# A third ring place for the shifted strips of the second convolution, and a second queue for their copies

## What is computed

```python
x = x + L0(gn(x))   # a 3x3 convolution of the 2-D Fourier transform, and back
x = x + L1(gn(x))   # rows of an image kept or dropped by the sign of a dot product
x = x + conv3x3(gn(x), W)         # "first convolution" in this text
x = x + conv3x3(gn(x), weight)    # "second convolution", the stage that is changed
```

## Time and profile before

| | us |
|---|---|
| median of three runs | 4663.69 |
| the profiled execution | 4668.15 |
| its span, from the first to the last instruction | 4666.4 |
| TensorE (PE) busy | 4247.7 (91%) |
| DVE busy | 2763.7 (59%) |
| ACT busy | 2637.1 (57%) |
| DMA queue q1 (SP's), share of the time of 16 DMA engines | 57.5% |
| DMA queue q10 (ACT's) | 0.3% |

### The profile page before, as it was taken

One profiled execution on the slowest core, in us unless ns is written; L12 is line 12 of the kernel. 1 busy time (PEld: TensorE's weight loads), 2 busy tenths in 40 slices (PEclk: granted clock), 3 DMA queues, 4 the chain that ended last, 5 costly groups with the idle time before them and its releaser, 6 DMA issues.

```text
span 4666.4 us, 172858 instructions
## 1 busy us (share of the span) xinstructions
PE 4247.7 (91%) x60064; PEld 2285.3 (49%) x60064; DVE 2763.7 (59%) x9972; ACT 2637.1 (57%) x7597; POOL 3.5 (0%) x22
## 2 busy tenths in 40 slices
PE   4999989999899998998999988999889999888786
PEld 1555436555355544555345543555435554355432
DVE  1677717775277743777357771777717775277730
ACT  4455655556555565555655565556555556544463
POOL 0000000000000000000000000000000000000000
PEclk8999899999999899999999999999899999999998
DMA  7443666646666566665666666565666547544376
GB/s 201 108 126 107 165 159 175 176 133 166 155 177 176 137 163 158 177 176 145 152 166 175 174 154 151 163 176 150 163 152 172 176 136 174 145 123 123 102 182 195
DMA packets 437852, 732.96 MB, mean 157 GB/s; under 512 B 42544, under 2 KB 109296, under 8 KB 437232
## 3 DMA queue, kind: packets, MB, share of 16 engines
q1 hardware_dynamic: 434544, 722.07, 57.5%
q10 hardware_dynamic: 2816, 4.20, 0.3%
HBM read 323.98 MB, written 134.22 MB: 98 GB/s over the span
## 4 chain that ended last, share of the span: by engine, by line
PE 83%; DMA 6%; SPq 3%; issue 3%; DVE 3%; ACT 1%; DVEq 0%; ACTq 0%
PE ps L1332 25%; PE ps L1250 20%; PE ps L1235 19%; PE ps L1243 6%; DMA shared<-x 5%; PE ps L1259 5%; PE ps L1109 5%; SPq L439 1%; SPq L469 1%; DMA x<-x 1%; PE ps L1357 1%; PE ps L1155 1%; PE ps L1156 0%; SPq L391 0%; PE ps L1182 0%
## 5 line engine op out<-in xcount | busy, mean ns | idle before, releaser
L1332 PE MATMUL ps<-x,conv_s 64*32 64x512 f32 x12288 | 1401.4, 609 | 141.6 <-DMA shared<-x 122.7
L1332 PE MATMUL ps<-shared,conv_s 64*32 64x512 f32 x12288 | 1410.3, 608 | 0.0
L638 ACT ACTIVATE x<-ps,vec 128x256 f32 (+1 forms) x1024 | 490.5, 495 | 1003.8 <-PE ps L1250 1003.8
L1250 PE MATMUL ps<-hil,shared 128*128 128x256 f32 x4096 | 993.6, 386 | 0.0
L1250 PEld LDWEIGHTS ps<-hil,shared 128*128 128x128 f32 x4096 | 740.4, 190 | 273.8 <-issue 194.1
L885 DVE SCALAR_TENSOR_TENSOR shared<-xin,trig 128x256 f32<-128x256 f32 x2048 | 823.5, 441 | 57.2
L1332 PEld LDWEIGHTS ps<-x,conv_s 64*32 64x32 f32 x12288 | 433.3, 108 | 757.6 <-issue 720.7
L713 ACT ACTIVATE x<-ps,vec 64x512 f32<-64x512 f32 (+1 forms) x768 | 525.5, 684 | 398.4 <-PE ps L1332 388.6
L1235 PE MATMUL ps<-shared 32*32 32x512 f32 x16384 | 662.8, 608 | 0.0
L897 DVE COPY vsb<-ps 128x512 f32<-128x512 f32 x512 | 329.9, 686 | 549.2 <-PE ps L1235 549.2
L1332 PEld LDWEIGHTS ps<-shared,conv_s 64*32 64x32 f32 x12288 | 490.6, 108 | 153.6 <-issue 143.6
(11 more groups left out here) (175 smaller groups left out, 3377.7 us busy)
## 6 DMA issues: line engine op xcount, KB each, us to landing
shared<-x SPq DMA_DIRECT2D x808, 256.0 KB, 5.0
xin<-x SPq DMA_DIRECT2D x512, 256.0 KB
out<-x SPq DMA_DIRECT2D x512, 256.0 KB
shared<-x SPq DMA_DIRECT2D x128, 768.0 KB, 6.2
shared<-x SPq DMA_DIRECT2D x496, 128.0 KB, 3.6
shared<-t_strip SPq DMA_DIRECT2D x512, 96.0 KB, 3.7
x<-x SPq DMA_DIRECT2D x64, 256.0 KB, 9.1
x<-t_proj SPq DMA_DIRECT2D x1, 2048.0 KB, 10.9
```

Source lines behind the costliest of these rows:

```text
L638: ins = nc.scalar.activation(split_in(strip_of(s))[:, q, :], split_in(ps[:, bank, :])[:, q, :], ACT.Identity, bias=v1(MEAN), accum_out=sum ...
L1250: mm = pe.matmul(split_in(ps[:, BY + 2 * odd + e, :])[:, int(q < 2), :], xt[:, e, q, :], hil[:, q, 0:HALF], start=False, stop=True, skip_g ...
L1332: mm = pe.matmul(ps[TM * cg:TM * cg + TM, banks[k], :], conv_s[rows, kw, kind, :], of, start=(kw == 0), stop=(kw == TAPS - 1), skip_group_ ...
```

## The change

The second convolution gets three places in the ring in place of two. The 16 groups are put into the places 0, 1, 2, 0, 1, 2 ... up to group 13; the last two take the places 0 and 1. So group g waits for the end of group g - 3, but group 14 for that of group 12 and group 15 for that of group 13. The DMA of 768 KB stays on SP's queue; that of 256 KB is now issued by ACT's queue, in `copy_rest`: for group 0 before the square root, for the groups 1 and 2 behind it, and for each later group behind the eviction of the last pair of the group whose place it takes. The loads of the next image's tables move on SP's queue from behind the copy of group 2 to behind that of group 15. In image 7, stores begin behind copy 3 in place of copy 2, and twelve stand at the end in place of eight.

```diff
-RING2, RING3 = 3, 2
+RING2, RING3 = 3, 3
+GROUPS3 = PAIRS // 2
+PLACES3 = tuple(g % RING3 for g in range(GROUPS3 - 2)) + (0, 1)
...
+        def place3(g):
+            return PLACES3[g], PLACES3[:g].count(PLACES3[g])
+        def freed3(g):
+            return max((k for k in range(g) if PLACES3[k] == PLACES3[g]), default=None)
...
-                if g >= RING3:
-                    sp.wait_ge(convolved, cv(i, 1 + PAIRS + 2 * (g - RING3) + 2))
+                if freed3(g) is not None:
+                    sp.wait_ge(convolved, cv(i, 1 + PAIRS + 2 * freed3(g) + 2))
                     sp.sem_inc(s_sp, 1)
-                if g == PAIRS // 2 - 1:
-                    sp.wait_ge(v_pads, i + 1)
-                    sp.sem_inc(s_sp, 1)
-                s, slot = BLOCKS * g, BLOCKS * (g % RING3)
...
-                sp.dma_start(ring[q3, slot:slot + BLOCKS, 1:1 + N], x1[q0, s + 1:s + 1 + BLOCKS, 1:1 + N]).then_inc(copied3[g % RING3], 16)
...
-                    if more and g == RING3:
+                    if more and g == GROUPS3 - 1:
...
+                def copy_rest(g):
+                    s, (place, _) = BLOCKS * g, place3(g)
+                    slot = BLOCKS * place
+                    if freed3(g) is not None:
+                        act.wait_ge(convolved, cv(i, 1 + PAIRS + 2 * freed3(g) + 2))
+                    if g == GROUPS3 - 1:
+                        act.wait_ge(v_pads, i + 1)
+                        act.sem_inc(s_act, 1)
+                    act.dma_start(ring[q3, slot:slot + BLOCKS, 1:1 + N], x1[q0, s + 1:s + 1 + BLOCKS, 1:1 + N]).then_inc(copied3[place], 16)
+                act.wait_ge(evicted, ev(i, 1 + STRIPS))
+                act.sem_inc(s_act, 1)
+                copy_rest(0)
                 root(i, 4, ZV)
+                for g in range(1, RING3):
+                    copy_rest(g)
...
                     evict3(n, banks3(n))
+                    for g in range(RING3, GROUPS3):
+                        if n == 2 * freed3(g) + 1:
+                            copy_rest(g)
```

More of the change, by code:

```diff
@@ L461, in copy3 @@
                     sp.sem_inc(s_sp, 1)
-                if g >= RING3:
-                    sp.wait_ge(convolved, cv(i, 1 + PAIRS + 2 * (g - RING3) + 2))
+                if freed3(g) is not None:
+                    sp.wait_ge(convolved, cv(i, 1 + PAIRS + 2 * freed3(g) + 2))
                     sp.sem_inc(s_sp, 1)
-                if g == PAIRS // 2 - 1:
-                    sp.wait_ge(v_pads, i + 1)
-                    sp.sem_inc(s_sp, 1)
-                s, slot = BLOCKS * g, BLOCKS * (g % RING3)
-                sp.dma_start(ring[0:P - TM, slot:slot + BLOCKS, 1:1 + N], x1[TM:P, s:s + BLOCKS, 1:1 + N]).then_inc(copied3[g % RING3], 16)
-                sp.dma_start(ring[q3, slot:slot + BLOCKS, 1:1 + N], x1[q0, s + 1:s + 1 + BLOCKS, 1:1 + N]).then_inc(copied3[g % RING3], 16)
+                s, (place, _) = BLOCKS * g, place3(g)
+                slot = BLOCKS * place
+                sp.dma_start(ring[0:P - TM, slot:slot + BLOCKS, 1:1 + N], x1[TM:P, s:s + BLOCKS, 1:1 + N]).then_inc(copied3[place], 16)
             def load_next(image, s, t, k):
@@ L1341, in outputs3 @@
                 def outputs3(s):
-                    turn, slot = 2 * (s % 2), s % (RING3 * BLOCKS)
+                    turn, slot = 2 * (s % 2), BLOCKS * place3(s // BLOCKS)[0] + s % BLOCKS
                     return ((turn, 0, None, 0), (2 - turn, 1, None, 0), (1 + turn, 0, slot, 0), (3 - turn, 1, slot, 0))
@@ L1397, in convolutions @@
                     if n % 2 == 0:
-                        pe.wait_ge(copied3[g % RING3], (i * (PAIRS // 2 // RING3) + g // RING3 + 1) * COPIES3 * 16)
+                        place, before = place3(g)
+                        pe.wait_ge(copied3[place], (i * PLACES3.count(place) + before + 1) * COPIES3 * 16)
                         due()
```

## The result

The changed kernel takes **4612.12 us** (median of 4 runs, 4609.66 to 4618.31), the kernel before 4665.16 beside it (4 runs): ratio 0.9884, 95% interval 0.9855 to 0.9912. It is faster by 53 us where the prediction had 88, and it lies 4 us above the top of the predicted range, 4608. The profiled execution took 4618.31 us (span 4616.5), the predicted 88.2 us would have made it 4580.0: **38.3 us are missing.** Both spans have a mean granted clock of 0.959.

The account below looks back on a forecast made before the run. TensorE was taken to bound images 0 to 6 except in waits for ring copies, and the DMA engines' busier half image 7. 88.6 - 4.9 + 4.5 = 88.2 us off 4663.7 gave 4575.5 us, range 4558 to 4608.

Parts of the forecast that it names:

- What bounds the kernel: Second convolution, images 0 to 6: TensorE bounds it except in waits for ring copies, which cost 108.2 us in all.
- the third place: Images 0 to 6: gaps of groups 2 to 13 go, 2.8 us an image stays, so 88.6 us are gained.
- DMA bandwidth suffices: Ring copies, images 0 to 6: 1.05 MB a group at 247 GB/s takes 4.25 of the 5.15 us available.
- The sum of 88.2: Whole kernel: 88.6 us gained in images 0 to 6, 4.9 lost at the stage's start, 4.5 gained in image 7.
- The groups 14 and 15: End of the second convolution: these keep a distance of two and wait 2.8 us an image, bounds 2.0 and 4.0.
- The clock behind the gap: Images 1 and 2: slow first pairs after gaps, 3.3 and 1.8 us, counted among the 108.2 us of gap cost.
- The start of the stage: First copies of the second convolution: the second small copy may share DMA engines, 0.7 us an image, 4.9 us lost.
- ACT's queue: 16 issues an image on ACT, 0.62 us each, fit between the evictions of a group; cost nothing.
- Image 7: Last image's second convolution: the busier half of the DMA engines bounds it; gain 4.5 us, bounds 0 and 10.
- The ring's term: Image 7: idle time of the first groups is saved, as one copy more is moved there; 4.5 us gained.
- the small copies wait behind SP's: Rival: ACT's issue stands behind SP's stores, costing groups 14 and 15 and the start 24 us; 4600 us, chance 0.15.

Follow-up runs that it names:

- ring_alone: The change, but with the small copy back on SyncE's queue behind the large one; 4592.39 us, ratio 0.9826 to the kernel before.
- ring_stores_late: Three places, both copies on SyncE's queue, large first, and the eight stores of images 0 to 6 behind copy 15; 4577.33 us, run again 4580.04.
- image7_sp: The change, with the small copies of image 7 alone back on SyncE's queue; 4601.54 us, ratio 0.9851 to the kernel before.

## Why the prediction was wrong

By its own steps:

- **What bounds the kernel, and the third place: right.** The gaps of the groups 2 to 12 went, evictions are 2.58 us apart there (three starts in a row at 648.52, 651.09, 653.67), and SyncE's copies with three places are the whole gain. "DMA bandwidth suffices" held even with a store a group. The kernel that has only the ring, without what disturbs the copies 12 to 15, gains 95.3 and 93.1 us in its two comparisons (4672.61 - 4577.33, 4673.13 - 4580.04). The sum of 88.2 was sized for such a kernel, and that it comes near is in part luck, since image 7 gives more than was taken and the groups 13 to 15 cost more.
- **The groups 14 and 15: wrong, +16.8 us.** The step that failed is "large and small together are still one stream of 1.05 MB, which lands some 7.0 us after that end", and under it "the issue falls 1.5 to 2.3 us after TensorE's end". ACT's sequencer issues under a running ACTIVATE, 0.06 us ahead of SyncE. That put the small copy first and the large one last, with stores behind it: it lands 8.0 to 9.8 us after its issue, where 7.0 after the freed group's end was taken. The upper bound given, 4.0 us an image, was for a late small copy; the large one was the late one, and 5.19 came of it. The order is not the whole of it: with the large copy first (ring_alone) a stage still takes 5.4 us over the 97.8 of one without gaps, where 2.8 was taken, and 3.4 with the stores moved as well; so "stores stand behind the large copy here" was sized too low too. The gaps also begin at group 13, whose copy has two stores ahead and two behind.
- **The clock behind the gap: left out, +11.0 us.** The prediction had counted slow pairs in two of the images of before (3.3 and 1.8 us) and put all of it among what goes. A gap of 3.6 to 5.3 us at group 14 brought 1.7 us of slow pairs in five of the images and 2.5 in one. The stop in image 3, +2.2 us, was foreseen by nothing.
- **The start of the stage: wrong the other way, 4.9 us too much.** ACT's first small copy is issued at 566.90 beside SyncE's large one at 566.89, and TensorE starts 6.83 us later, as before (567.20 to 574.04); the pause of TensorE ahead of the stage is 8.7 to 8.8 us in all images of both kernels. The copies of the groups 1 and 2 on ACT's queue, from 569.63 on, delay nothing that is waited for. By the Trainium skill's rule of turns ("DMA: Bandwidth & Descriptors", section "Queues, rings and completion order") 1.1 us an image, the prediction's estimate, should have gone here; in this start it isn't seen, and why isn't settled.
- **ACT's queue: right in its own cost.** Issues are 0.61 us in the median, and ACT was never the bound.
- **Image 7: wrong in sign, 10.4 us.** The ring's term was right in direction and small: 166.2 to 156.2 with SyncE's queue, 10.0 where 4.5 was taken (0 to 10 given), by a single execution of before. What the prediction lacked is that its second half touches image 7 at all: 12 us back. It asked who waits behind ACT's issues, and not what SyncE does with the time that it no longer needs for the small copies.
- **The rival "the small copies wait behind SP's"** was the reverse of what happened; its 4600 came nearest only by size.

Split by the runs, the images 0 to 6 lose 733.9 - 708.3 = 25.6 us against the best kernel: 14.4 by the stores behind the copies 12 to 15 (722.7 - 708.3), 8.4 by the small copy being first (731.1 - 722.7), and 2.8 that is left (733.9 - 731.1), of which 2.2 are the stop in image 3. So in these images no cost of the second queue itself is shown. The split depends on the way taken: with the small copy on ACT's queue, moving the stores is worth 20.3 (733.9 - 713.6). With image 7's 12 us, the small copy's move to ACT's queue costs 23 us in all, against the 20 to 30 by which the times of the change and of ring_alone differ.

Open: why such a pair is complete some 2 us later when the small copy is first (9.2 and 9.3 us in the mean of group 14, against 7.3), and why less so without stores behind it (7.7 against 7.4). The trace's packets don't name the transfer they belong to. The Trainium skill ("DMA: Bandwidth & Descriptors", section "Queues, rings and completion order") says that of one queue a later transfer may be done before an earlier one; no landing of these pairs shows it, since both copies count up one semaphore and the stores' landings are not in the trace. Nor did I find what decides whether the clock falls: pairs are slow behind gaps of 2.8 us in ring_alone (images 1 and 2) and not behind gaps of 3.6 us in ring_stores_late (images 0, 4 and 5).

## What to carry to other kernels

A pair of transfers is worth its last landing: when you move one to another queue, ask which of the two is now last and what is queued behind it, and issue the large one first. A queue that is relieved of work runs ahead to its next limit, here the program's four stores in flight, and takes what stands behind that limit with it, so cost the relieved queue as carefully as the one that gets the work. Put stores behind the copies that have time to spare, not behind those whose distance is short.

## What was not expected of the hardware

- A DMA that stands in ACT's program behind the three ACTIVATEs of an eviction leaves 0.01 us after the first of them has started and 0.7 us before the second, for the groups 3 to 14 of all eight images, and takes 0.60 us.
- With the small copy of 256 KB first and two stores behind, the pair of group 14 was complete 9.2 us after its first issue in the mean of seven images; with the large one of 768 KB first, 7.3. It made hardly a difference whether the small one was on another queue (9.2) or on the same (9.3).
- The Trainium skill ("DMA: Bandwidth & Descriptors", section "Issuing engines are not separate DMA queues") says that issuing from several engines saves only the sequencer's time of the issue. In the images 0 to 6 the runs agree: with the same order, two queues cost 2.8 us more than one in seven images, of which the unexplained stop is 2.2. In image 7 they show a loss: 212 GB/s from one queue (image7_sp), 189 from two (the change).
